# Rotation tables for four heads at a time, and kernel numbers stored from their columns

## The reference

```
dtA = A * dt[:, None];  Cs = Cc * (exp(dtA) - 1) / A
K   = 2 * einsum('hn,hnl->hl', Cs, exp(dtA * arange(L))).real
y   = causal_conv(u * mask, K) + u * mask * D;   y *= mask
logits = y @ route_w.T;  top value v at expert e
out = x + v * ((y @ A[e].T) @ Bw[e].T)
```

## Time and profile before

| | |
|---|---|
| three runs | 622.61, 623.76, 623.93 us (median 623.76) |
| profiled execution | 623.93 us, of which the span from first to last instruction is 622.1 us |
| PE, PEld busy | 95%, 85% of the span |
| DVE, ACT, POOL busy | 87%, 61%, 60% |
| granted TensorE clock, mean | 0.992 of full speed |
| DMA moved | 77.68 MB |

### The profile page before, as it was taken

How to read it: one execution, slowest core, us unless ns; L and a number is a source line. 1 busy time by engine, 2 the same in 40 slices (tenths; PEclk the granted TensorE clock), 3 DMA queues, 4 the chain that set the end, 5 groups by cost and what they waited for, 6 DMA issues and landing times.

```text
span 622.1 us, 13886 instructions
## 1 busy us (share of the span) xinstructions
PE 591.5 (95%) x3681; PEld 530.9 (85%) x3681; DVE 542.5 (87%) x1436; ACT 379.3 (61%) x1164; POOL 372.9 (60%) x474
## 2 busy tenths in 40 slices
PE   3379999999999999999999999999999999999995
PEld 2268998999899889988998998899899989988984
DVE  7778889988988898899889888988998898889874
ACT  3676656766676666567666766665676667666520
POOL 4465566557656755675576567556755765676520
PEclk9989999999999999999999999999999999999998
DMA  6023534453454345435534543454345345434521
GB/s 137 17 56 108 152 110 128 147 150 96 142 149 132 113 139 153 112 126 146 152 96 139 151 133 110 141 152 114 125 146 152 98 136 151 139 105 140 154 78 67
DMA packets 37074, 77.68 MB, mean 125 GB/s; under 512 B 11836, under 2 KB 20350, under 8 KB 36998
## 3 DMA queue, kind: packets, MB, share of 16 engines
q1 hardware_dynamic: 27846, 43.76, 29.5%
q10 hardware_dynamic: 9152, 33.03, 13.0%
HBM read 43.16 MB, written 33.62 MB: 123 GB/s over the span
## 4 chain that ended last, share of the span: by engine, by line
PE 92%; DVE 4%; issue 2%; POOL 1%; ACT 0%; DMA 0%; POOLq 0%
PE psYo L987 19%; PE psZ L1009 19%; PE psO L987 15%; PE psYe L987 12%; PE psS L987 11%; PE psO L1036 5%; PE psXe L1000 4%; PE psXo L1000 4%; PE psZ L1078 1%; PE psS L1047 1%; DMA logs<-in_L_cond_log_dt_dram 0%; DVE ex L693 0%; POOL Grev L436 0%; POOL wave L426 0%; DVE fraction L803 0%
## 5 line engine op out<-in xcount | busy, mean ns | idle before, releaser
L468 POOL TENSOR_TENSOR Slo<-Sf,Shi 128x384 fp32r<-128x384 f32 x64 | 64.9, 1015 | 210.1 <-ACT Shi L590 210.1
L852 DVE SCALAR_TENSOR_TENSOR brought<-Sf,tab,psS 64x128 f32<-64x128 f32 x256 | 89.0, 348 | 47.3 <-ACT Sf L585 40.9
L1009 PE MATMUL psZ<-Wt,Y 128*128 128x136 f32 x1024 | 129.6, 280 | 0.0
L1009 PEld LDWEIGHTS psZ<-Wt,Y 128*128 128x128 f32 x1024 | 127.8, 191 | 0.1
L531 ACT ACTIVATE Ghi<-Grev 128x256 fp32r<-128x256 f32 x64 | 26.8, 418 | 94.2 <-POOL Grev L436 94.2
L884 DVE TENSOR_TENSOR ost<-psO,xt 128x512 f32<-128x512 f32 x128 | 82.0, 676 | 2.2 <-PE psO L987 2.2
L461 POOL TENSOR_TENSOR Xlo<-xeven,Xhi 128x512 fp32r<-128x512 f32 x64 | 82.8, 1293 | 0.0
L568 ACT ACTIVATE Xhi<-psXe 128x512 fp32r<-128x512 f32 x64 | 38.2, 597 | 38.3 <-PE psXe L1000 38.3
L789 DVE TENSOR_SCALAR whole<-turns_t 128x256 f32<-128x256 f32 x64 | 57.8, 903 | 4.1 <-ACT turns_t L519 4.1
L585 ACT ACTIVATE Sf<-psS 128x128 f32<-128x128 f32 x64 | 17.7, 277 | 66.4 <-PE psS L987 66.4
L987 PE MATMUL psYo<-Xhi,Thi 128*128 128x512 f32 x128 | 55.6, 434 | 0.0
(11 more groups left out here) (194 smaller groups left out, 1670.8 us busy)
## 6 DMA issues: line engine op xcount, KB each, us to landing
xt<-in_x_dram SPq DMA_DIRECT2D x64, 512.0 KB, 4.1
out_dram<-ost ACTq DMA_DIRECT2D x63, 512.0 KB, 4.8
Traw<-kdram SPq DMA_DIRECT2D x64, 128.0 KB, 2.9
kdram<-krow SPq DMA_DIRECT2D x64, 1.0 KB
A_nat<-in_L_ffn_A_dram SPq DMA_DIRECT2D x1, 512.0 KB, 4.9
B_nat<-in_L_ffn_Bw_dram SPq DMA_DIRECT2D x8, 64.0 KB, 3.6
out_dram<-ost SPq DMA_DIRECT2D x2, 256.0 KB, 2.0
lens_i<-in_itok_B_dram SPq DMA_DIRECT2D x1, 64.0 KB, 3.6
```

The lines of the kernel that those rows point to most:

```text
L468: pool.tensor_tensor(Slo[h.s2][:, :], Sf[h.s2][:, :], Shi[h.s2][:, :].bitcast(F32), ALU.subtract).then_inc(slo_done, 1)
L852: dve.scalar_tensor_tensor(brought[to, :], Sf[h.s2][fr, old], tab2[fr, BR, h.n:h.n + 1], psS[to, new], ALU.mult, ALU.add).then_inc(brought ...
L1009: last = pe.matmul(psZ[:, 0:NW], Y[:, j, c, :], Wt[:, 2 * c + j, :], start=(j == 0 and c == 0), stop=(j == 1 and c == NE - 1), skip_group_ ...
```

## The change

The tables are made for parts of four heads. The 256 angles of a mode are split into 16 coarse and 16 fine ones; per part POOL computes the steps (`angle_steps`, three small products), ACT four `turns` of 128x64, DVE and POOL the fractions, ACT one `sines`, POOL three products with the magnitudes (`weigh`), ACT four copies from one half of the partitions to the other (`mirror`). Per head POOL then makes `Grev` from an outer product of 512 numbers (`both`) and one sum of 256. The work of a part is put into steps whose number is divisible by four (`angle_steps`, `weigh`, `mirror`), or leaves 1 (`turns`, `whole_turns`), 2 (`turn_parts`, `fractions`, `clamp`) or 3 (`sines`).

From head 3 on `turn_k` and `k_row` fall away: SP writes the two columns of `kcol` straight to memory, 256 pieces of 4 bytes, and reads back the table one step later. PE's order becomes bring, turn_x, inputs, project, within, turn_wh, from_states, up. `carry` works in psS and not in `brought`; `rank` of the gates lies in psZ. ACT's step begins with `store` and `t_hi`; POOL's with `t_lo`, the parts and `g_table`. The work before the loop is reordered, and step 0 is written out in it; the Exp of the magnitudes is done for 8 heads there and for 56 in step 2.

```diff
             def write_kernel(h):
 
-                need(sp, krow_done, h.n + 1)
                 need(sp, t_in[h.s2], h.half * 16)
...
+                else:
+                    need(sp, kcol_done, h.n * 2 + 2)
+                    with nc.allow_non_contiguous_dma(reason="kernel numbers stand on the partitions"):
+                        sp.dma_start(bass.AP(kdram.tensor, h.s2 * (P + Q), [[1, P], [P, 2]]),
+                                     kcol[h.s2][:, :]).then_inc(k_out[h.s2], 16)
...
+            def angle_steps(part):
...
+                for t, table in ((step_h, VH), (step_t, V), (step_l, VL)):
+                    pool.tensor_tensor(t[:, 0:part.n, :],
...
+            def weigh(part):
...
+                for table, half, size in ((coarse, 0, COARSE), (fine, 0, FINE), (fine, 1, FINE)):
+                    pool.tensor_tensor(table[:, half, part.heads, :], wave[:, size, 0:part.n, :],
+                                       mag[:, size, part.heads, :], ALU.mult).then_inc(weighed, 1)
...
                 pool.tensor_tensor(
+                    both[:, :, :, :],
+                    coarse[:, :, h.n, :].rearrange("p t (a b) -> p t a b", b=1).to_broadcast(wide),
+                    fine[:, :, h.n, :].rearrange("p t (a b) -> p t a b", a=1).to_broadcast(wide),
+                    ALU.mult).then_inc(both_done, 1)
...
+                pool.tensor_tensor(Grev[h.s2][:, :], both[:, 0, :, :].rearrange("p a b -> p (a b)"),
+                                   both[:, 1, :, :].rearrange("p a b -> p (a b)"), ALU.add).then_inc(grev_done, 1)
...
             def step(head):
-                if head(0).there and not is_head(head(0), 0):
+                if head(0).there and not is_head(head(0), 1):
+                    t_lo(head(0))
+                if part_at(head(8)):
+                    angle_steps(part_at(head(8)))
+                if part_at(head(6)):
+                    turn_parts(part_at(head(6)))
+                if part_at(head(4)):
+                    weigh(part_at(head(4)))
+                if head(3).there and not is_head(head(0), 1):
+                    g_table(head(3))
+                if head(0).there:
                     s_lo(head(0))
...
             def step(head):
-                if head(0).there and not is_head(head(0), 0):
+                if head(-2).there:
+                    store(head(-2))
+                if head(0).there and not is_head(head(0), 1):
+                    t_hi(head(0))
+                if head(0).there:
                     first_state(head(0))
...
-                        dve.scalar_tensor_tensor(brought[to, :], Sf[h.s2][fr, old],
+                        dve.scalar_tensor_tensor(psS[to, new], Sf[h.s2][fr, old],
```

More of the change, by code:

```diff
@@ L262, in __init__, with part_at @@
                 self.there = 0 <= n < H
+        class Part:
+            def __init__(self, k, start, stop):
+                self.k = k
+                self.start = start
+                self.n = stop - start
+                self.heads = slice(start, stop)
+        EDGES = list(range(0, H + 1, FIRST))
+        parts = [Part(k, EDGES[k], EDGES[k + 1]) for k in range(len(EDGES) - 1)]
+        def part_at(h):
+            for part in parts[2:]:
+                if part.start == h.n:
+                    return part
+            return None
         def is_head(h, *numbers):
@@ L332, in step @@
                     write_kernel(head(2))
-                    skew_kernel(head(2))
+                if head(1).there and not is_head(head(0), 1):
+                    skew_kernel(head(1))
             load_x(Head(0))
@@ L348, in _ @@
             load_x(Head(1))
+            load_x(Head(2))
             sp.wait_ge(pad_done, 32)
-            for n in range(2):
+            for n in range(3):
                 write_kernel(Head(n))
@@ L422, in g_table @@
             def g_table(h):
-                need(pool, wave_done, h.n + 1)
+                need(pool, mirrored, 4 * sum(part.start <= h.n for part in parts))
                 need(pool, grev_done, h.n)
+                wide = [P, 2, G16, G16]
                 pool.tensor_tensor(
[L427 to L430, removed]
@@ L522, in sines, with turns @@
[L522 to L525, removed]
+            def turns(part):
+                need(act, steps_done, part.k * 3 + 3)
+                need(act, frac1_done, part.k)
+                need(act, whole_done, part.k)
+                for size, scale in ((COARSE, float(G16)), (FINE, 1.0)):
+                    act.activation(turns_h[:, size, 0:part.n, :], step_h[:, 0:part.n, :], ACT.Identity,
+                                   scale=scale, bias=quarter[:, :]).then_inc(turns_done, 1)
+                    act.activation(turns_t[:, size, 0:part.n, :], step_t[:, 0:part.n, :], ACT.Identity,
+                                   scale=scale, bias=quarter[:, :]).then_inc(turns_done, 1)
@@ new lines, in sines, with magnitudes @@
+            def sines(part):
+                need(act, frac_done, part.k + 1)
+                need(act, weighed, part.k * 3)
+                act.activation(wave[:, :, 0:part.n, :], fraction[:, :, 0:part.n, :], ACT.Sin,
+                               scale=TURN).then_inc(wave_done, 1)
+            def magnitudes(heads):
+                act.activation(mag[:, COARSE, heads, :], rho16[:, heads, :], ACT.Exp,
+                               scale=float(G16)).then_inc(mag_done, 1)
+                act.activation(mag[:, FINE, heads, :], rho16[:, heads, :], ACT.Exp).then_inc(mag_done, 1)
@@ new lines, in mirror @@
+            def mirror(part):
+                need(act, weighed, part.k * 3 + 3)
+                top, low = slice(0, N), slice(N, P)
+                for table, to, half, fr, scale in ((coarse, low, 1, top, 1.0), (coarse, top, 1, low, -1.0),
+                                                   (fine, low, 0, top, 1.0), (fine, top, 1, low, 1.0)):
+                    act.activation(table[to, half, part.heads, :], table[fr, half if table is fine else 0, part.heads, :],
+                                   ACT.Copy, scale=scale).then_inc(mirrored, 1)
@@ L636, in _ @@
             act.activation(sine_half[:, :, :], phase[:, :, :], ACT.Sin, scale=TURN / 2).then_inc(sines_done, 1)
[L637 to L644, removed]
+            turns(parts[0])
+            act.wait_ge(rho_done, 1)
+            magnitudes(slice(0, 2 * FIRST))
+            sines(parts[0])
+            for dst, src in weights():
+                act.wait_ge(w_turned, 1)
+                act.activation(dst, src, ACT.Copy).then_inc(w_done, 1)
+            mirror(parts[0])
             act.wait_ge(tabs_turned, 2)
-            act.activation(tab2[:, :, :], psY[1][:, 0:5 * H].rearrange("p (t h) -> p t h", h=H),
+            act.activation(tab2[:, :, :], psX[0][:, 0:5 * H].rearrange("p (t h) -> p t h", h=H),
                            ACT.Copy).then_inc(tab_done, 1)
@@ L973, in _ @@
                    Bw_hi[:, j * 512:(j + 1) * 512].bitcast(F32), ALU.subtract).then_inc(blo_set, 1)
-            dve.wait_ge(mask_done, NB)
-            dve.wait_ge(tab_done, 2)
+            b_lo(first[0])
+            masks(0, 4)
+            dve.wait_ge(tab_done, 2)
+            carry(first[0])
+            x_lo(first[1])
+            b_lo(first[1])
+            masks(4, NB)
+            whole_turns(parts[1])
+            dve.wait_ge(mask_done, NB)
+            b_lo(first[2])
+            cut(first[0], 0)
+            cut(first[0], 1)
+            fractions(parts[1])
+            clamp(parts[1])
             run_steps(step)
@@ L1043, in turn_k, with within @@
                 need(pe, krow_done, h.n)
-                if h.n < 2:
-                    need(pe, *((xlo_odd, 1) if h.n else (xeven_done, 1)))
-                need(pe, s_carried, (h.n - 1) * 2)
-                pe.transpose(psK(h), kcol[h.s2][:, :], ident[:, :]).then_inc(k_turned, 1)
-            def within(h, j, behind):
+                pe.wait_ge(w_done, 3)
+                pe.transpose(psK(), kcol[h.s2][:, :], ident[:, :]).then_inc(k_turned, 1)
+            def within(h, j):
                 need(pe, thi_done, h.n + 1)
@@ L1102, in step @@
                     turn_x(head(1), 1)
-                if head(2).there and not is_head(head(0), 0):
+                if head(2).there:
                     inputs(head(2))
+                if head(-1).there:
+                    project(head(-1))
                 if head(0).there:
-                    within(head(0), 0, None)
-                    within(head(0), 1, head(-1))
-                if is_head(head(0), 0):
-                    inputs(head(2))
-                if head(2).there:
-                    turn_k(head(2))
-                if is_head(head(0), H):
+                    within(head(0), 0)
+                    within(head(0), 1)
+                if head(-1).there:
                     turn_wh(head(-1))
@@ L1123, in turn_tables @@
                 last.then_inc(tabs_turned, 1)
-            first = [Head(n) for n in range(2)]
-            pe.wait_ge(consts, 10)
```

(16 more changed lines are left out.)

323 lines of the change are left out of this document (154 added, 169 removed).

## The result

The changed kernel took 799.85 us (median of 4 runs, 794.6 to 805.07) against 623.18 for the kernel before beside it: a ratio of 1.283, 95% interval 1.2753 to 1.2907. The forecast was 620.2 us. The profiled execution took 803.35 us, with a span of 800.4.

A forecast was written before the change was run, and what follows sets the result against it. PE was taken to bound the loop from end to end. Transposes -6.7, POOL +7.3, gates +2.9, tail -0.7 and start -6.5 sum to -3.7 us, from 623.93 to 620.2 us; range 611 to 628.

The forecast's parts named there:

- The 4-byte pieces: SP's write of 256 pieces per head and its read-back: each at most 3.6 us, hidden by the step, cost 0.
- rival 4: The 4-byte write is slow and `t_hi` waits for the table; 61 us per us past the slack; chance 0.05.
- Well beyond the dearest row: The case in which the 4-byte write would show: a transfer far slower than the 3.6 us taken.
- POOL in every fourth step: In 13 steps (4 to 52) POOL's queue makes `s_lo` 0.56 us late for PE: +7.3 us (2.5 to 14.6).
- the cover of `mirror`: ACT's `mirror` falls between `g_hi` and `w_hi`, when ACT otherwise waits for PE; costed at nothing.
- The gates: DVE's gates after `carry` and `x_lo`, with PSUM operands, make `wh` 0.06 us late in 48 steps: +2.9 us (0 to 6.2).
- rival 3: Gates reach PE late because `gate` is held by POOL's `s_lo` in every step: 16 to 32 us; chance 0.11.
- The tail: In the last steps `gate`, with `rank` in PSUM, is no longer held by `s_lo`: -0.7 us once.
- The start: Before the loop one part serves four heads, taking two heads' table chains off, less `mirror`: -6.5 us (-3.7 to -9.1).
- The transposes: PE's transposes of the kernel numbers go for 61 heads, 0.11 us each: -6.7 us.

The follow-up runs named there:

- swap: The changed kernel with the 4-byte write kept and SP's read-back of the next head put ahead of the write of the head after it; 782.52 us, ratio 1.2568.
- the run with rows: The changed kernel with all heads' kernel numbers again turned by PE and written from two rows, read-back ahead of the write; 627.91 us, ratio 1.0074.

## Why the prediction was wrong, point by point

**The 4-byte pieces: the step that failed.** The forecast bounded the write by the loads of B at 3.6 us, "hidden, 0". Those are reads of 64-byte pieces; the nearest row was not near. Writing 4-byte pieces side by side took 9.6 us to complete, and the read-back, bounded by the same 3.6, took 9.0 though it moves what it moved before. The slack I had counted for the read was right: 8.9 - 2.4 - 0.5 = 6.0 us. So rival 4 is what happened, and its price, 61 us for each us past the slack, comes close: (9.0 - 6.0) x 61 = 183 us. Measured: 799.85 - (627.91 - 6.7) = 179. It had a chance of 0.05, on the strength of rows 8 alone. "Well beyond the dearest row" was the case that had to be held open: no row showed a write of single numbers, and the two ends should have been far apart.

That what stands beside the write is late too, I had not considered at all. The Trainium skill, "DMA: Bandwidth & Descriptors", section "Queues, rings and completion order", has a transfer's semaphore increment land only after every earlier write of the same DMA engine, across its queues. The runs fit it: the read-back behind the write moved its bytes in 2.9 us and landed after 9.0, and stores from the other queue landed after 8.6 instead of 5.1. The read of `swap`, issued ahead of the write and held for 9.82 us all the same, that sentence does not tell by itself, and no run settles it. The Trainium skill, same page, section "Specifications", has a DMA below 512 bytes read, modify and write; here that by itself was cheap, as 64-byte pieces and 4-byte pieces 16 bytes apart completed within 3.3 us.

The other terms are read from the run with rows, where the write is gone. Its chain, around a step with a part of four tables (L1125 and L1152 are the two transposes):

```profile
322.31 0.11 PE psS L1125
322.42 0.11 PE psZ L1152
322.53 0.53 PE psYe L1065 x3
...
324.99 1.05 PE psS L1065 x6
...
331.53 0.40 issue
331.93 0.77 PE psYe L1065 x3
332.70 0.52 PE psYo L1065 x3
333.22 1.59 PE psO L1065 x6
334.81 1.05 PE psS L1065 x6
```

and ACT and POOL in that step:

```profile
325.75 0.37 ACTq L651 DMA_DIRECT2D out_dram<-ost  x1
326.22 0.42 ACT L635 ACTIVATE Thi<-Traw 128x256 fp32r<-128x256 f32 x1 [3.13 <-DVE ost L966]
```

```profile
326.71 0.73 POOL L495 TENSOR_TENSOR Tlo<-Traw,Thi 128x256 fp32r<-128x256 f32 x1 [2.98 <-ACT Thi L635]
327.40 0.29 POOL L444 TENSOR_TENSOR step_h<-tab,grid 128x64 f32<-128x64 f32 x1
...
328.99 1.06 POOL L471 TENSOR_TENSOR both<-coarse,fine 128x512 f32<-128x512 f32 x1
...
330.83 1.00 POOL L510 TENSOR_TENSOR Slo<-Sf,Shi 128x384 fp32r<-128x384 f32 x1
```

**POOL in every fourth step: right, and dearer.** `Thi` starts 326.22 - 324.99 = 1.23 us into the step (forecast 1.33), `t_lo` at 1.72 (1.76), `s_lo` ends at 6.84 (6.82); the small instructions are 0.29 to 0.32 (0.31). Exactly the thirteen steps 4 to 52 are long, 9.82 us against 8.99: 0.83 each, 10.8 us in all, where I had 7.3 and an upper end of 14.6. The wait itself is 0.40, plus the 0.11 that the transpose gives back here; the forecast's 0.56 was that. (The ten instructions have nine joins, not eight, 0.04 less.) What it left out follows behind: the first group after the stall takes 0.77 instead of 0.53, and `up` 1.59 instead of 1.40. For `up`, ACT's queue says why: the four copies of `mirror` run from 331.35 to 332.44 and, in this run but not in the changed kernel, `k_row` to 332.59 ahead of `w_hi`, so that `wlo` ends only at 333.07, and PE's first weight load for `up` follows at 333.14:

```profile
331.35 0.53 ACT L597 ACTIVATE coarse<-coarse 64x64 f32<-64x64 f32 x2
331.90 0.54 ACT L597 ACTIVATE fine<-fine 64x64 f32<-64x64 f32 x2
332.34 0.25 ACT L629 ACTIVATE krow<-psS 2x128 f32<-2x128 f32 x1
332.50 0.25 ACT L668 ACTIVATE whi<-psZ 128x128 fp32r<-128x128 f32 x1
...
332.78 0.29 DVE L950 TENSOR_TENSOR wlo<-psZ,whi 128x128 fp32r<-128x128 f32 x1 [1.53 <-ACT whi L668]
...
333.14 0.19 PEld L1065 LDWEIGHTS psO<-Bw_hi,whi 128*128 128x128 f32 x1 [0.24 <-issue]
```

That is the cover of `mirror`, priced at nothing, gone; how much of the 0.19 is `k_row`'s, no run tells apart.

**The gates: +2.9 forecast, nothing found.** PE waited for `wh` in three steps (the start and the tail), 3.0 us in all, and the plain step is 8.99 us with the transpose in it. The groups of DVE (busy us, mean ns; idle before) in the run with rows:

```profile
L916 DVE TENSOR_SCALAR gate<-psZ,best,top 128x8 f32<-128x8 f32 x64 | 18.2, 284 | 2.5 <-DVE best L910 0.3
...
L910 DVE TENSOR_REDUCE best<-psZ 128x1 f32<-128x8 f32 x64 | 10.7, 167 | 2.2
```

`gate` took 284 to 288 ns in all 64 heads (mean before 302), so rival 3 falls with its premise, and `best` from PSUM 167 against 153: the 0.014 us of the forecast, and not the 0.065 worked out there from the Trainium skill, "VectorE: DVE Perf Modes", section on the TRN2 errata. **The tail:** from the last `bring` to the end 627.12 - 608.56 = 18.56 us, before 622.13 - 602.36 = 19.77: -1.2, forecast -0.7.

**The start: right in kind, smaller.** The second `bring` began at 36.85 (changed kernel: 36.55; forecast near 36), but the step behind it took 12.40 us, longer than before. At the third, 49.25 against 53.52, -4.3 of the forecast's -6.5, inside its range. In that long step the tables of the second part of four heads stand in the way: ACT's `sines` (`wave`) starts at 39.66 after waiting 1.96 us for DVE's `fraction`, the four copies of `mirror` follow at 41.18, and only then `Sf`, at 42.18. That is 5.33 us into the step, where it is 326.54 - 324.99 = 1.55 in the step shown above, and PE waits 1.23 us for `wh` at its end. The forecast had taken two heads' chains off and put nothing there.

**The transposes:** with the store moved and the turn done by DMA, the span fell from 615.5 to 609.2, -6.3 (by the medians of the runs -5.9); forecast -6.7.

Sum for the run with rows, by span: -4.3 + 10.8 - 1.2 - 0.3 (48 plain steps a few ns shorter) = +5.0, from 622.1 to 627.1. The forecast had +3.0 for these terms. All but 2 us of the miss is the one term, the write that was put at 0.

## What to carry to other kernels

A write of single numbers side by side has a price of its own: bound it by no read and by no wider piece, and if the trace has no such write, let the range say so. Ask what else is in flight when a slow transfer completes, since independent loads and stores can land late with it, though their bytes moved long before. When numbers must turn from partitions into a row, do it where small pieces are cheap (here by DMA within the on-chip memory) and write the row to memory in long pieces.

## What was not expected of the hardware

- One transfer of 256 pieces of 4 bytes, written side by side in memory, completes after 9.6 to 10.1 us, one of 128 after 8.9; 256 pieces 16 bytes apart, 3.3; into the on-chip memory in two transfers, 2.7 each.
- A 512 KB load issued at 49.85, 2.9 us ahead of such a write (52.73), landed 12.51 us after its issue in the changed kernel; before, such loads took 4.1 at the median.
- After stalls PE can pay again. In the step behind `Thi` at 317.28 it waited 2.96, 1.11 and 0.61 us, and then `up` ran 2.65 us instead of 1.40. The view by stretch has the granted clock there at 0.52, its lower level of 1.2 GHz; in the step before, with waits of 1.24 and 1.11, it stayed at 1.00 (the rows from 309 to 312 above). Over the span it averaged 0.954, and 0.996 in the run with rows:

```profile
324.00:327.00 3.00, 3.00 (x9) 2.38 (x8) 1.89 (x4) 0.00 (x0) 0.82 (x2) 0.52 0.00 0
```
